# Selective-scan layer: row groups outside and states inside, with two of four turned state tiles added by DMA

## The reference

```
xm, z = split(h @ W_in)                  # 512 time steps x 1024 channels each
xm    = silu(causal conv of 4 taps (xm))
dtr, B, C = split(xm @ W_xp)             # 64, 16 and 16 columns
dt    = softplus(dtr @ W_dt + b_dt)
for every state s of 16:
    h_s[t] = h_s[t-1] * exp(dt[t] * A_s) + dt[t] * xm[t] * B_s[t]
    y[t]  += C_s[t] * h_s[t]
y = (y + xm * D) * silu(z)
out = y @ W_out, times a gate, gathered by itok and added to x
```

## Time and profile before

| | |
|---|---|
| median of 3 runs | 3429.93 us (3427.78 to 3430.2) |
| profiled execution, its own time | 3433.88 us |
| its span (first to last instruction) | 3431.8 us |
| PE / DVE / ACT / POOL busy over the span | 2870.9 / 2457.3 / 1598.1 / 1818.9 us |
| mean granted TensorE clock | 0.902 |
| scans L1639 | 1024, 1209 ns each |
| state sums L1680 | 800, 729 ns each |

### The profile page before, as it was taken

How to read it: one execution, slowest core, us unless ns; L and a number is a source line. 1 busy time by engine, 2 the same in 40 slices (tenths; PEclk the granted TensorE clock), 3 DMA queues, 4 the chain that set the end, 5 groups by cost and what they waited for, 6 DMA issues and landing times.

```text
span 3431.8 us, 32982 instructions
## 1 busy us (share of the span) xinstructions
PE 2870.9 (84%) x11066; PEld 1600.0 (47%) x11066; DVE 2457.3 (72%) x3184; ACT 1598.1 (47%) x2252; POOL 1818.9 (53%) x771
## 2 busy tenths in 40 slices
PE   7999999999999987677887887887887887877765
PEld 3545454554545443345445445445445444444442
DVE  3444444444444244999999999999999999999992
ACT  1122122222212215576576676676675675675550
POOL 0121111112111111779689689689689689688791
PEclk9999999999999997887997987987987988988887
DMA  5002020110202222332354354353353353353362
GB/s 189 7 25 80 0 79 24 55 55 24 79 0 80 74 81 72 65 74 68 68 120 99 75 118 93 77 118 92 77 120 89 77 126 86 81 128 87 87 135 62
DMA packets 193879, 270.05 MB, mean 79 GB/s; under 512 B 16877, under 2 KB 82545, under 8 KB 193738
## 3 DMA queue, kind: packets, MB, share of 16 engines
q1 hardware_dynamic: 146152, 183.53, 16.8%
q0 software_dynamic: 44032, 83.91, 14.3%
q10 hardware_dynamic: 3554, 0.88, 0.2%
HBM read 167.32 MB, written 42.22 MB: 61 GB/s over the span
## 4 chain that ended last, share of the span: by engine, by line
DVE 23%; PE 15%; issue 11%; POOL 8%; ACT 4%; DMA 1%; DVEq 0%; POOLq 0%; ACTq 0%
DVE hs L1639 13%; DVE acc L1680 7%; PE bank L1209 5%; PE bank L1152 4%; POOL hs L1516 3%; PE bank L1235 3%; POOL dt L1498 1%; DVE xm L1607 1%; PE bank L1182 1%; ACT bank L1394 1%; PE bank L1176 1%; POOL acc L1535 1%; POOL fin L1526 1%; POOL u L1506 1%; PE bank L1216 1%
## 5 line engine op out<-in xcount | busy, mean ns | idle before, releaser
L1516 POOL TENSOR_TENSOR hs<-u,b_wide 128x2048 f32<-128x2048 f32 x256 | 1280.8, 5026 | 75.4 <-DVE u L1631 75.2
L1639 DVE TENSOR_TENSOR_SCAN hs<-bank,hs 128x512 f32<-128x512 f32 x1024 | 1226.4, 1209 | 23.6 <-ACT bank L1394 15.6
L1209 PE MATMUL bank<-ident,hs 128*128 128x128 f32 x4096 | 751.4, 319 | 351.2 <-DVE hs L1639 228.9
L1394 ACT ACTIVATE bank<-dt,decay 128x512 f32<-128x512 f32 x1024 | 697.8, 689 | 623.2 <-DVE hs L1639 617.6
L1209 PEld LDWEIGHTS bank<-ident,hs 128*128 128x128 f32 x4096 | 561.2, 163 | 888.6 <-DVE hs L1639 397.1
L1680 DVE SCALAR_TENSOR_TENSOR acc<-bank,c_t,acc 128x512 f32<-128x512 f32 x800 | 583.0, 729 | 91.4 <-PE bank L1209 80.7
L1152 PE MATMUL bank<-h_t,w_in 128*128 128x512 f32 x1024 | 546.9, 622 | 8.8 <-ACT h_t L1325 4.4
L1535 POOL DMA_DIRECT2D acc<-scaled x224 | 254.4, 1136 | 314.8 <-ACT scaled L1401 313.7
L1235 PE MATMUL bank<-w_y,zs 128*128 128x512 f32 x512 | 261.3, 601 | 3.5 <-DVE fin L1697 2.5
L726 POOL TENSOR_TENSOR y_rs<-y_var,mhalf 128x8 f32<-128x8 f32 x8 | 16.0, 2004 | 440.4 <-DVE y_var L200 440.4
L585 PE MATMUL bank<-z_t,w_k 128*128 128x512 f32 x512 | 221.8, 594 | 5.9 <-ACT z_t L682 5.9
(11 more groups left out here) (154 smaller groups left out, 3086.6 us busy)
## 6 DMA issues: line engine op xcount, KB each, us to landing
acc<-scaled POOLq DMA_DIRECT2D x224, 256.0 KB, 4.0
w_in<-in_L_cond_W_in SPq DMA_DIRECT2D x128, 256.0 KB, 3.8
b_wide<-b_rows SPq DMA_DIRECT2D x128, 256.0 KB, 3.7
z<-in_x SPq DMA_DIRECT2D x8, 2048.0 KB, 8.3
res<-in_x SPq DMA_DIRECT2D x8, 2048.0 KB, 8.6
x_rows<-res SPq DMA_DIRECT2D x7, 2048.0 KB, 7.4
fin<-x_rows SPq DMA_DIRECT2D x56, 256.0 KB, 2.7
out<-fin SPq DMA_DIRECT2D x56, 256.0 KB
```

The source lines that it names most:

```text
L1209: last = nc.tensor.transpose(state_banks[n % len(state_banks)][:, j * P:(j + 1) * P], hs[:, q % RING, j, t * P:(t + 1) * P], ident[:, :])
L1394: nc.scalar.activation(decay_bank(k)[:, :], dt[:, par, j, :], ACT.Exp, scale=g.decay[:, j, s:s + 1]).then_inc(da_ready, 1)
L1516: nc.gpsimd.tensor_tensor(hs[:, q % RING, :, :], u[:, 4 * half:4 * half + 4, :], b_wide[:, s % 2, :].unsqueeze(1).to_broadcast([P, 4, CHUNK]),
L1639: nc.vector.tensor_tensor_scan(block, decay_bank(k)[:, :], block, 0.0, ALU.mult, ALU.add).then_inc(scanned, 1)
```

## The change

- **Order.** Row groups outside, states inside: a turn is now two *half-turns* of 16 units, first states 0 to 15 of row groups 0 to 3, then of groups 4 to 7. Units and blocks are numbered through all batches (`U`, `N`), and ACT and POOL run over the border of two turns. Only one half of dt, of dt*xm and of `acc` is in use at a time. So the dt of the second half is prepared at the start of its own turn (blocks 0 to 16), the first half of the next batch at blocks 86 to 101, sums 0 to 3 are turned out from block 105 on and 4 to 7 in the next turn. `dt*xm` overwrites `xm` in three rotating `slots`; `u` is gone.
- **Tiles.** DVE adds tiles 0 and 1 of a unit (`DVE_TILES` = 2, one block later than before, `LAG`). ACT scales tiles 2 and 3 into one buffer, and POOL issues one accumulating DMA of 512 KB, after `inputs(U)` for unit U-4, when the DMA before it has landed. Only the last four units of the whole kernel (`DIRECT`) are added wholly by DVE.
- **Banks.** The decays have 3 banks throughout, the work 3 (`h`, `xm`, `z`, `dt`, `y`, `init`, `out` share them). W_in products are issued in three steps, (0,1), (2), (3), the output product in six.
- **Loads.** B is loaded for each unit (256 loads of 256 KB, a ring of 4), since a state comes back in the second half.
- **End.** In the last turn z and the first four groups of three output tiles are computed ahead; after the last unit four sums go to four banks of their own. The final rows of batch 6 use `g.rows` as buffers.

The diff, cut:

```diff
 RING = 4
-BLOCKS = STATE * KI
-HALVES = BLOCKS // 4
+UNITS = 2 * STATE
+BLOCKS = 4 * UNITS
 W_IN_RING = 4
+B_RING = 4
 SCALED_RING = 2
-DVE_TILES = CT - 1
-SHARED = HALVES - RING
-SUMS = DVE_TILES * SHARED + CT * (HALVES - SHARED)
-FOUR_BANKS = 60
-assert FOUR_BANKS % 3 == 0 and (BLOCKS - FOUR_BANKS) % 4 == 0
-
-
-def work_order(*stages):
-
-
-    uses, seen = {}, {}
-    for stage, n in stages:
-        for _ in range(n):
-            i = seen.get(stage, 0)
-            uses[stage, i], seen[stage] = len(uses), i + 1
-    return uses
-
-
-
-FRONT = work_order(("h", KD), ("xm", KI), ("xd", 1), ("C", 1), ("dt", KI))
-PREPARE = (("h", KD), ("xm", KI), ("z", 1), ("xd", 1), ("z", 2), ("C", 1), ("dt", 4), ("z", 2), ("dt", 4), ("z", 3))
-FIRST_TURN = work_order(("init", KI), *PREPARE)
-TURN = work_order(*[("y", 1), ("init", 1)] * KI, *PREPARE)
-LAST_TURN = work_order(*[("y", 1), ("init", 1)] * KI, ("z", KI))
-END = work_order(("y", KI))
-
-CHUNK_ORDER = work_order(("h", KD), ("xm", KI), ("xd", 1), ("C", 1), ("dt", KI), ("init", KI), ("z", KI), ("y", KI))
-
-
-def turn_place(b):
-
-    first = len(FRONT) // 2
-    if isinstance(b, int) and b == 0:
-        return first, FIRST_TURN
-    start = first + len(FIRST_TURN) // 2 + len(TURN) // 2 * (b - 1)
-    return start, LAST_TURN if isinstance(b, int) and b == BATCH - 1 else TURN
+DVE_TILES = 2
+LAG = 1
+SLOTS = 3
+DIRECT = BATCH * UNITS - 4
...
+DT_AT = (86, 87, 91, 92, 0, 1, 5, 6)
+Y_AT = (105, 107, 111, 113, 9, 13, 17, 20)
+INIT_AT = (106, 108, 112, 114, 10, 14, 18, 21)
+H_AT = (15, 19, 22, 23)
+OUT_AT = (24, 36, 45, 54)
+XM_AT = (30, 33, 42, 51, 60, 63, 66, 69)
+XD_AT = 78
+C_AT = 88
+Z_AT = (72, 75, 84, 93, 96, 99, 115, 118)
+
+LAST_OUT_AT = (24, 30, 36, 42)
+LAST_Z_AT = (48, 51, 54, 57, 60, 63, 66, 69)
+LAST_Y_AT = (76, 78, 80, 82, 9, 13, 17, 20)
+LAST_OUT_HALF_AT = (96, 102, 108)
+
+ROWS_SPLIT = ((0, 1), (2,), (3,))
...
+def tiles_of(U):
+    return DVE_TILES if U < DIRECT else CT
...
-        xm = sb("xm", [P, KI, CHUNK])
+        slots = sb("slots", [P, SLOTS, 4, CHUNK])
         zs = sb("zs", [P, KI, CHUNK])
-        dt = sb("dt", [P, 2, KI, CHUNK])
-        u = sb("u", [P, KI, CHUNK])
-        acc = sb("acc", [P, CT, INNER])
+        dt = sb("dt", [P, 2, 4, CHUNK])
+        acc = sb("acc", [P, 2, CT, 512])
         hs = sb("hs", [P, RING, 4, CHUNK])
-        b_wide = sb("b_wide", [P, 2, CHUNK])
+        b_wide = sb("b_wide", [P, B_RING, CHUNK])
         c_t = sb("c_t", [P, 2, CT, STATE])
-        scaled = sb("scaled", [P, SCALED_RING, 512])
+        scaled = sb("scaled", [P, SCALED_RING, CT - DVE_TILES, 512])
...
-        state_banks, out_bank, work_banks = banks[0:2], banks[2], banks[6:8]
+        state_banks, decay_banks, work_banks = banks[0:2], banks[3:6], [banks[6], banks[7], banks[2]]
...
+        def state_read(U, t):
+
+            if t < tiles_of(U):
+                return summed, sums_before(U) + t + 1
+            return state_scaled, (CT - DVE_TILES) * U + t - DVE_TILES + 1
+
+        def pooled(U):
+
+            return state_pooled, DMA * min(U, DIRECT)
...
+                    need(pe, scanned, 4 * (U + 1))
+                if t >= 2:
+                    need(pe, *state_read(U, t - 2))
+                elif U > 0:
+                    need(pe, *state_read(U - 1, t + 2))
+                states_to(state_banks[t % 2], U % RING, t)
...
+            def y_turned(place, j):
+                U = UNITS * place.it + STATE * (j // 4 + 1)
+                need(pe, summed, sums_before(U))
+                need(pe, *pooled(U))
...
+                need(pe, summed, sums_before(UNITS * BATCH))
+                for j in range(4):
+                    sums_turned(end_banks[j], 4 + j).then_inc(end_turned, 1)
+                pe.wait_ge(end_gated, 4)
+                place = PLACES[BATCH - 1]
+                for t in range(CT - 1):
+                    project_out(place, t, range(4, KI))
+                project_out(place, CT - 1, range(KI))
...
+            def decays(N):
+
+                U, j = N // 4, N % 4
+                H, s = U // STATE, U % STATE
+                if N % (4 * STATE) == 0:
+                    need(act, dt_ready, H + 1)
+
+                need(act, scanned, N - 2)
+                nc.scalar.activation(decay_banks[N % 3][:, :], dt[:, H % 2, j, :], ACT.Exp,
+                                     scale=g.decay[:, 4 * (H % 2) + j, s:s + 1]).then_inc(da_ready, 1)
...
+            def scale_state(U, t):
+
+                need(act, turned, CT * U + t + 1)
+                need(act, *pooled(U - SCALED_RING + 1))
+                nc.scalar.activation(scaled[:, U % SCALED_RING, t - DVE_TILES, :], state_banks[t % 2][:, :], ACT.Copy,
+                                     scale=c_t[:, U // UNITS % 2, t, U % STATE:U % STATE + 1]).then_inc(state_scaled, 1)
+
...
+                    if N + 3 < BLOCKS * BATCH:
+                        decays(N + 3)
+                    if 0 <= U < DIRECT and n % 4 >= DVE_TILES:
+                        scale_state(U, n % 4)
...
+                    if n == 2 and prev:
+                        silu_z(PLACES[b - 1], 1)
...
+                    if n == 12:
+                        exp_dt(place, 1)
+                    if n == 16:
+                        log_dt(place, 1)
...
-            def pool_state(it, q):
-
-                t, jg = CT - 1, q % 2
-                part = acc[:, t, jg * 512:(jg + 1) * 512]
-                apart(pool, state_scaled, SHARED * it + q + 1)
-                apart(pool, state_pooled[jg], DMA * (SHARED // 2 * it + q // 2))
-                nc.gpsimd.dma_start(part, scaled[:, q % SCALED_RING, :], accum_op=ALU.add).then_inc(state_pooled[jg], DMA)
-
-            def turn(b, par, prev, more):
-                for q in range(HALVES):
-                    if q >= RING:
-                        pool_state(b, q - RING)
-                    inputs(b, q)
...
+            def pool_state(U):
+
+                need(pool, state_scaled, (CT - DVE_TILES) * (U + 1))
+                need(pool, *pooled(U))
+                nc.gpsimd.dma_start(acc[:, U // STATE % 2, DVE_TILES:, :], scaled[:, U % SCALED_RING, :, :], accum_op=ALU.add).then_inc(state_pooled, DMA)
...
+                for s in range(UNITS):
+                    U = UNITS * b + s
                     if more:
-                        if q == 1:
-                            gather(b + 1, b + 1, 0)
-                        if q == 4:
+                        if s == 3:
+                            gather(b + 1)
+                        if s == 5:
                             rows_rsqrt(nc, g, b + 1)
                             next_rows(b + 1)
-                        if q == 24:
-                            add_dt(b + 1, 1 - par, 0)
-                        if q == 29:
-                            add_dt(b + 1, 1 - par, 1)
-                    if prev and 20 <= q < 20 + NT:
-                        if q == 20:
+                    inputs(U)
+                    if U >= RING:
+                        pool_state(U - RING)
+                    if s == 7:
+                        add_dt(2 * b + 1)
+                    if s == 11:
+                        dt_x(2 * b + 1)
+                    if more:
+                        if s == 28:
+                            add_dt(2 * b + 2)
+                        if s == 31:
+                            dt_x(2 * b + 2)
+                    if b >= 2:
+                        for k, at in ((5, 2), (6, 4), (7, 6)):
+                            if s == at:
+                                add_y(b - 2, k, chunk_of_y(b - 2))
...
+            def added_at(U, step):
+
+                lag = LAG if U < DIRECT else 0
+                return (step - lag,) if U >= 0 and 0 <= step - lag < tiles_of(U) else ()
...
+                before, after = PLACES[b - 1] if prev else None, PLACES[b + 1] if more else None
+                for n in range(BLOCKS):
+                    N, U = BLOCKS * b + n, UNITS * b + n // 4 - 1
+                    scan(N)
+                    for t in added_at(U, n % 4):
+                        add_states(U, t)
+                    for j, at in enumerate((111, 113, 117, 119, 15, 19, 23, 26) if more else (82, 84, 86, 88, 15, 19, 23, 26)):
+                        if n == at and (j < 4 or prev):
+                            gate_y(place if j < 4 else before, j)
+                    if prev:
```

966 lines of the change are left out of this document (558 added, 408 removed).

## The result

The changed kernel takes 3351.86 us (median of 4 runs, 3347.91 to 3354.19) against 3428.86 for the kernel before (3424.99 to 3430.2): a ratio of 0.9776, interval 0.9759 to 0.9793. It is 77 us faster. The forecast was 3258, and the range went from 3175 to 3345: the time lies above it. The profiled execution took 3353.27 us, its span is 3351.4.

The account below looks back on a forecast made before the run. DVE was taken to bound the kernel, at 255 us a turn. Savings of 136 (seven turns), 10.5 (beginning), 11 (last turn) and 14 (end) made 172 us, so 3258 us; range 3175 to 3345.

Parts of the forecast that it names:

- the gain of the steady turn: Steady turns: 215.5 us of DVE work plus 10, 5 and 5 of waits, 235.5 us, 19.5 less than 255.
- 36 sums leave VectorE, 23 us a turn: DVE, each turn: 100 sums become 64, 36 x 0.64 = 23.0 us, work falling from 238.5 to 215.5.
- PE, 5 us: Turned tiles coming late from PE, at low clock and behind output products: 5 us a turn, bounds 0 and 15.
- ACT blocks, 10 us: Scans waiting while ACT does table load, silu or logarithm, table load: 10 us a turn, bounds 0 and 18.
- POOL, 5 us, and the DMA inside it: POOL at 210 us of work a turn, running late: 5 us, bounds 0 and 19; landing 5.6 us inside it.
- the rival with a landing of 8 us: Slower: accumulating DMA runs in series, landing by proportion after 8 us, turns of 270 us, 3500 us; chance 0.08.
- Sum: Each turn 215.5 + 10 + 5 + 5 = 235.5 us, 19.5 less than 255; seven turns: 136 us.
- Beginning and end: First scan 10.5 us earlier; fewer last turned sums and output products ahead make the end 14 us shorter.
- Last turn, 11 us less: Last turn, taken as 212 us: loses 28 sums (18 us), gets 4 gates and about 5 us of waits.
- POOL becomes the bound: Rival: landing of 7 us or issue of 0.9 us, turns of 246 to 248 us, 3342 us; chance 0.20.
- No new waits: Rival: ACT blocks fall behind taps and PE keeps full clock, turns of 223 us, 3170 us; chance 0.17.
- the drain: Rival: each ACT table switch holds 1.38 us longer than its row, 22 us more a turn, 3410; chance 0.01.

Follow-up runs that it names:

- ring 4: The changed kernel with SCALED_RING 4 in place of 2 (four scaled buffers for ScalarE's tiles): 3333.22 us, ratio 0.9715.

## Why the prediction was wrong, step by step

The step that failed is the gain of the steady turn: 23 us of VectorE's work a turn, kept but for 20 us of waits. The runs show that the second tile gave nothing in the changed kernel (the turn with three tiles is as long), and that the gain of the turns needs a number in the diff that the sum doesn't hold, LAG. That the kernel is faster, as forecast, is to this extent luck.

- *36 sums leave VectorE, 23 us a turn.* Right as work (213.9 against 215.5 us forecast), wrong as time. "This is the gain of the change" is the sentence that failed: with three tiles on VectorE the turn is the same 245 us. In the new order VectorE's work is no longer what a turn costs: of 241 us more taken off it, 40 show. (Four of the 36 sums leave with the new order, whatever the tiles.)
- *PE, 5 us.* Mis-sized, and the step that missed the gain. Sums wait 13.6 us for tiles, partly because ScalarE, held by its ring, gives TensorE's banks back late: ring 4 took 48 us of these waits off the trace. And the 12.3 us of late tiles were read as TensorE's clock and its long products, and the change as moving them about. LAG, each sum one scan later, was not priced. By the ratios it is worth 74 us with three tiles and 70 with two, and takes the waits before sums from 15.3 to 1.8 and from 30.0 to 13.8 us a turn. The reading of the clock was not wrong: the earlier trace rows don't carry it, as VectorE works 7.84 of 8 us at the low clock too, but in the trace before 76 of some 90 us of late tiles stand before tiles that took TensorE over 0.9 us (0.60 at full clock, 1.12 at low). A sum that comes a scan of 1.13 us later hardly sees such a tile.
- *ACT blocks, 10 us.* The mechanism was right and the size was near: scans wait 14.9 us, nearly all behind table loads, and 6.7 with three tiles, where VectorE has more sums in hand. But the waits don't add to a bound that lies elsewhere: 17 us of 3333 came back when all table loads were taken out, 93 us when GpSimd's products were shorter as well (3290 to 3197).
- *POOL, 5 us, and the DMA inside it.* The work of 210 us was right (209.2), issuing 512 KB as cheap as 256 KB was right, a landing of 5.6 us nearly (6.0). The wait at the issue was named, and put inside the 5 us; it is 12.2 us a turn on top of 209 of work, as GpSimd issues only between products of 4.8 us and only when the former DMA is down. What the sum put at nothing is ScalarE's wait: it stood only in the rival with a landing of 8 us. With a ring of two ScalarE waits for the same landings at 6.0, 18.5 us a turn, with decays queued behind. The ring alone cost 19 us of time, the second load of B 34 to 45.
- *Sum.* Seven turns and what follows, by the starts of the scans: forecast 136 us less in seven turns, measured 73.9 (1779.7 to 1705.8).
- *Beginning and end.* 15.6 us for 10.5, 15.8 for 14. Right in kind; the step left GpSimd's first product where it was, and it began 5 us earlier as well (at 1338.93 for 1343.99; the scans that wait for it 4.68 us start at 1343.53).
- *Last turn, 11 us less.* Wrong in sign. From its first scan to the last one it takes 241.4 us where it took 216.5: 24.9 us more. (The prediction's 212 us rest on seven turns of 255; the last turn began at 3138.7, not at 3144.) Before, VectorE was busy for 209 of its last 212 us; now it waits in that turn 28.3 us for tiles and 10.5 for decays, ScalarE 29.8 and GpSimd 13.3 for DMAs. With ring 4 the turn takes 232.5 us and with three tiles 222.5: 9 of the 25 us were the ring. So the miss of some 91 us (80.4 for 172) is 62 in seven turns and 36 in the last, less 5 and 2 at beginning and end.
- *The rivals.* "POOL becomes the bound", 3342, named one of the two bounds and came within 10 us of the time, but by a landing of 7 us that was 6.0, and without the later sums; that closeness is partly luck. The mark that the forecast set for it, 10 us a turn or more of GpSimd's issues waiting for DMA, is met (12.2). "No new waits" and the drain are out: the trace after has no gap of 1.38 us beside its table loads, and taking all table loads out, alone, brought 17 us. The landing in proportion (8 us) did not come either. (The drain's 3410 us would have been faster than before, and was counted in the chances as slower.)

Shown is: in the turns, nothing is gained without the later sums, and in the old order they bring 21 us of the 77. The second tile's 23 us were not kept because a turn then has two bounds near 240 us, VectorE behind ScalarE's in-order blocks, and GpSimd with products, issues and landings in one row. With ring 4 two tiles are 17 us faster in all than three tiles with ring 2; three tiles with ring 4 were not run. Not shown is what in the new order lets the later sums work, and why a mix of two and three tiles is slower than either.
